# Idle-slot products on TensorE in a sequential GRU stage

## What is computed

```python
# layer 1: state space, 32 states, 320 steps in sequence
state = tanh(state @ A_bar.T + ub_t)
# layer 2: gated recurrent unit, 256 hidden values, 320 steps in sequence
z = sigmoid(xz_t + h @ Wwz.T + bwz)
r = sigmoid(xr_t + h @ Wwr.T + bwr)
c = tanh(xc_t + (h * r) @ Ww.T + bw)
h = z * h + (1 - z) * c
out = sigmoid(hs @ Wo.T + bo)
```

## The kernel before, in words

| j | work behind the candidate's products |
|---|---|
| 0, 4, 6, 15 | none (in the first chunk 4 has `skip`) |
| 1, 13 | `ssm_input`: 64 columns, float32 |
| 2, 3 | `output_product` for the chunk before (L1280): 128 columns, float32 |
| 5 | `transpose_x2`: 128 columns, float32 |
| 7 to 12 | `gate_inputs` for the next chunk (L1127): 128 columns, float32; 11 and 12 first wait for the candidate's tanh of this step (`c_done`), since they write its bank |
| 14 | `ssm_out` (L1116): 128 columns on 32 rows, float32 |

## Time and profile before

### The profile page before, as it was taken

How to read it: one execution, slowest core, us unless ns; L and a number is a source line. 1 busy time by engine, 2 the same in 40 slices (tenths; PEclk the granted TensorE clock), 3 DMA queues, 4 the chain that set the end, 5 groups by cost and what they waited for, 6 DMA issues and landing times. The chain is left out here.

```text
span 996.5 us, 40786 instructions
## 1 busy us (share of the span) xinstructions
PE 890.0 (89%) x17497; PEld 735.9 (74%) x17497; DVE 512.9 (51%) x3153; ACT 359.1 (36%) x1673; POOL 87.8 (9%) x228
## 2 busy tenths in 40 slices
PE   7299999999989989989989989989989989998875
PEld 4156565766878878878878878878878878887765
DVE  2314243522555565555555555565555655655654
ACT  3236444522333333333333333333333333333322
POOL 2102021410000000000000000000000000000000
PEclk9999999985555555555555555555555555555555
DMA  3200000000000000000000000000000000000000
GB/s 101 88 1 2 1 1 1 1 1 1 3 3 6 6 3 6 6 3 6 6 4 6 6 4 6 6 4 5 6 3 6 6 3 6 6 3 6 7 3 8
DMA packets 7321, 8.62 MB, mean 9 GB/s; under 512 B 1112, under 2 KB 6426, under 8 KB 7140
## 3 DMA queue, kind: packets, MB, share of 16 engines
q1 hardware_dynamic: 6833, 6.00, 2.1%
q0 software_dynamic: 256, 0.01, 0.0%
q10 hardware_dynamic: 50, 0.00, 0.0%
HBM read 4.70 MB, written 1.31 MB: 6 GB/s over the span
## 5 line engine op out<-in xcount | busy, mean ns | idle before, releaser
L1266 PE MATMUL ps<-h_hi,w_first 128*128 128x8 f16 x2560 | 268.8, 171 | 61.1 <-DVE h_hi L386 61.1
L1266 PEld LDWEIGHTS ps<-h_hi,w_first 128*128 128x128 f16 x2560 | 223.2, 105 | 109.3 <-DVE h_hi L386 109.3
L1266 PE MATMUL ps<-h_hi,w_rest 128*128 128x8 f16 x5120 | 276.8, 168 | 0.0
L1266 PEld LDWEIGHTS ps<-h_hi,w_rest 128*128 128x128 bf16 x5120 | 242.5, 105 | 2.4
L734 ACT ACTIVATE tanh_r<-ps 128x16 f32<-128x16 f32 x320 | 58.6, 183 | 304.0 <-PE ps L1272 304.0
L1272 PE MATMUL ps<-h_lo,w_first 128*128 128x8 f16 x2560 | 159.9, 168 | 0.1
L972 DVE SCALAR_TENSOR_TENSOR rh_hi<-tanh_r,hseq 128x16 f16<-128x16 f32 x320 | 58.4, 183 | 185.3 <-ACT tanh_r L734 185.3
L1266 PE MATMUL ps<-rh_hi,w_rest 128*128 128x8 f16 x2560 | 139.0, 168 | 0.0
L1266 PE MATMUL ps<-rh_hi,w_first 128*128 128x8 f16 x1280 | 136.9, 173 | 2.2 <-DVE rh_hi L972 0.4
L386 DVE TENSOR_TENSOR_SCAN h_hi<-coef,addend 128x32 f16<-128x32 f32 x320 | 72.1, 225 | 105.3 <-ACT addend L744 105.3
L1266 PEld LDWEIGHTS ps<-rh_hi,w_rest 128*128 128x128 bf16 x2560 | 122.1, 105 | 0.0
(11 more groups left out here) (183 smaller groups left out, 1234.4 us busy)
## 6 DMA issues: line engine op xcount, KB each, us to landing
x_sb<-in_x SPq DMA_DIRECT2D x4, 500.0 KB
out<-res SPq DMA_DIRECT2D x20, 64.0 KB, 2.0
W_sb<-in_L_tok_W SPq DMA_DIRECT2D x1, 637.6 KB
W_sb<-in_L_tok_W SPq DMA_DIRECT2D x1, 384.0 KB
wnat<-in_L_ffn_Wwr SPq DMA_DIRECT2D x1, 256.0 KB, 4.1
wnat<-in_L_ffn_Wwz SPq DMA_DIRECT2D x1, 256.0 KB, 3.1
wnat<-in_L_ffn_Ww SPq DMA_DIRECT2D x1, 256.0 KB, 4.8
dft_sb<-in_dft SPq DMA_DIRECT2D x1, 157.8 KB
```

The lines of the kernel that those rows point to most:

```text
L1266: mm(gate(c, j, g, m), w[:, m * 128:(m + 1) * 128], state[:, k * NB:(k + 1) * NB], start=False, stop=False, skip_group_check=True)
```

## The change

At the end of every step's loop body, after the work of the table above, TensorE issues one more product: identity (bfloat16) as weights, `w_first` as the moving operand, into PSUM bank 1, which nothing reads in the scan. At `j` = 0, 4, 6 and 15 it has 512 columns, at the other twelve positions 128. It waits for nothing and signals nothing.

```diff
 SEED_AT = 1
+KEEP_BUSY_AT = 0, 4, 6, 15
 LAST_ROWS_AT = 2
...
                     if scan_2 and j == CH - 2:
                         ssm_out(c + 2, False)
+                    if j in KEEP_BUSY_AT:
+                        mm(bank(1), ident_bf[:], w_first[:, 0].rearrange("p k h -> p (k h)"), start=True, stop=True)
+                    else:
+                        mm(bank(1, 128, 128), ident_bf[:], w_first[:, 0, 0, 0:128], start=True, stop=True)
```

## The result

The changed kernel takes 1010.18 us (median of 12 executions, 1001.96 to 1015.05), the kernel before beside it 1002.98 (12 executions, 991.19 to 1010.98). The ratio is 1.0097, 95% interval 1.0056 to 1.0138: slower by 0.6 to 1.4%, as forecast in sign; the sum of +6.4 us is 0.64% of that base. The ratio is one of means over fast runs only (within 1.5% of the fastest of the same kernel), which leaves out the two slowest of the twelve before; the ratio of the medians of all twelve is 1.0072. In absolute time the forecast of 1014.8 stood on a median of three that was 5 us above the median of twelve.

What follows compares the result with a forecast made beforehand. The prediction took 320 rounds of one dependent ring across TensorE, ScalarE and VectorE to bound the kernel at half clock. Terms of 4.1, 1.9 and 0.4 us gave +6.4 on the 1008.35 median: 1014.8 us, range 957 to 1022.

Steps and rivals of the forecast that it cites:

- as forecast in sign: Whole kernel: slower was the likeliest outcome at 0.42, against faster 0.29 and same 0.29.
- the sum of +6.4 us: Added time over the scan at 1.2 GHz: 4.1 + 1.9 + 0.4 us, with bounds of 0 and 17 us.
- the forecast of 1014.8: Whole kernel: the added 6.4 us put on the timed median of 1008.35 us; chance 0.56.
- The clock: TensorE's granted clock in the scan: claimed to stay at 0.50 throughout, the added products being too thin to raise it.
- Rivals A and B: Full clock through the scan, 961 us, chance 0.18; or full clock in stretches, about 988 us, chance 0.12.
- The ring: All 320 scan steps: VectorE's `h_hi` waits for ScalarE's tanh, TensorE's next product for `h_hi`; a plain step takes 2.28 us.
- Positions 0, 4, 6, 15, and 1, 5, 13: Steps with enough free TensorE time, 0.70 us at the first four, to hide the added product: cost 0.
- `skip` once 0.43: First chunk, position 4: `skip` comes ahead of the 512-column product, so its whole 0.43 us counts once.
- Positions 11 and 12: Steps where TensorE is already late behind the candidate's tanh: 0.107 us exposed in full, 2 x 19 times, 4.1 us.
- Position 14: Step whose next product is already late, 0.41 us after the scan began: 0.107 exposed in full, 18 times, 1.9 us.
- Positions 2, 3, 7 to 10: 128 columns behind a wide float32 pair: slack 0.11 us against 0.107 needed, just fits, cost 0; bound 11 us.
- rival C: Weights not loaded ahead at the six tight positions: about 0.1 us more each, +17 us in all, 1026 us; chance 0.09.

## Why the prediction was right

*The clock.* Held: 0.50 in both profiles of the change from the scan's third step on. Rivals A and B fell. The reason was weaker than the forecast, and in part luck. It took from one execution that a dense float32 stretch stays at 0.50 and that the clock rose behind the three 512-column products. (Of the 89 products of that stretch, 24 are of 8 columns, so "nearly all wide" holds for their time and not for their number.) In the kernel before itself such work had full clock some microseconds earlier:

```profile
200.00:212.00 12.00, 12.00 (x71) 7.73 (x70) 2.43 (x7) 4.01 (x14) 0.22 (x1) 1.00 0.01 1
```

And in the repeat of the kernel before the clock rose in the midst of that stretch, ahead of the three products, which start at 240.07:

```profile
220.10:233.60 13.50, 13.50 (x48) 9.57 (x47) 2.45 (x10) 3.06 (x11) 2.36 (x5) 0.50 0.00 0
233.70:239.30 5.60, 5.60 (x37) 3.84 (x36) 0.56 (x1) 1.98 (x7) 0.00 (x0) 1.00 0.00 0
```

So that stretch did not tell what the scan would be granted. That the change's products are too little is shown by the runs: one, two and four products of 512 columns at every position stay at 0.50 too. What the prediction cited from the Trainium skill (TensorE: Matmul & The Clock Gate, "Why this matters for your kernels"), that back-to-back products keep the clock up, agrees with the run with eight and not with the run with four, where the engine was busy 594.50 of 600 us and the clock was 0.50.

*The ring.* "Every one of the 320 steps" reads too much into the earlier trace rows: TensorE's wait for `h_hi` stands there 147 times. At 11, 12 and 14, as the prediction says further on, TensorE's own earlier work ends last.

*Positions 0, 4, 6, 15, and 1, 5, 13.* Forecast 0, measured 0 within the 0.007 by which two executions of the kernel before differ; `skip` once 0.43, as forecast. (0.70 − 0.43 leaves 0.27, not 0.25.)

*Positions 11 and 12.* Forecast 38 x 0.107 = 4.1, measured 2.740 against 2.633: 4.1.

*Position 14.* Forecast 18 x 0.107 = 1.9, measured 2.500 against 2.393: 1.9. The first product is only 0.08 later there, unrounded, and the row behind it makes up the rest.

*Positions 2, 3, 7 to 10.* Forecast 0 and rival C 0.1 each. Measured 0.006 to 0.020, together 0.09 a chunk or 1.7 us; against the repeat of the kernel before, 0.06 a chunk or 1.1. This term was too small. 0.11 of slack held the product's 0.107 as far as the first product of the next step went; I left out those behind it. Half the width removes it.

The terms give 4.1 + 1.9 + 0.4 + 1.7 = 8.1 of the 8.6 us, and with 1.1 in place of 1.7 they give 7.5, where the two repeats differ by 7.4; the rest is of the size by which the kernel before differs from itself. So the forecast of +6.4 was 1.0 to 2.2 us short in the scan, while its base was 5.4 us too high: that 1014.8 lies within 5 us of 1010.18 is partly chance.

## What to carry to other kernels

Where a ring of dependent steps sets the time, filling an idle engine is free only up to the moment when it is wanted again; read that slack position by position, and look at every product behind the first. Before filling TensorE for its clock, measure which filling holds full clock and whether it fits the idle time: here the one that did hold it cost 0.90 us a step, where full clock without it would save 0.11. Here the positions where the engine was already late were worth more than the idle ones: taking one wait away there saved 13 us.

## What the runs showed of the hardware that was not expected

TensorE's busy share does not tell its clock: at 594 busy us of 600 it ran at 0.50 in one kernel and at 1.00 in another, and in the kernel before it stayed at 0.50 for 24.30 busy us. Filling more made the kernel faster, 1359.9 us with eight products against 1446.2 with four (one execution each), since the clock held. Full weights in place of identity changed nothing (scan 1187.8 against 1187.9). And the granted clock ahead of the scan differs from one execution of the same instructions to the next, and with it the time at which the scan begins, by up to 16 us.
